# A gather ring of eight blocks whose slots also hold the relation one-hots

## The reference

```python
x = x + _L0_gnn_ref(_layernorm(x), relvectors, w_ih, w_hh, b_ih, b_hh, src, dst, edge_type_16)
x = x + _L0_ffn_ref(_layernorm(x)[None], ...)[0]
x = x + _L1_gnn_ref(_layernorm(x), W, b, edge_index)
x = x + _L1_ffn_ref(_layernorm(x)[None], ...)[0]
```

## Time and profile before

| what | us |
|---|---|
| median of three runs | 3529.81 |
| the profiled execution's own time | 3538.93 |
| its span, first to last instruction | 3537.4 |
| setup, to the first gather | 143.0 |
| layer 0, first to last gather | 143.0 to 1587.5 |
| layer 1, first to last gather | 1691.1 to 2716.2 |
| from the last gather to the end | 821 |

### The profile page before, as it was taken

How to read it: one execution, slowest core, us unless ns; L and a number is a source line. 1 busy time by engine, 2 the same in 40 slices (tenths; PEclk the granted TensorE clock), 3 DMA queues, 4 the chain that set the end, 5 groups by cost and what they waited for, 6 DMA issues and landing times. The chain is left out here.

```text
span 3537.4 us, 56704 instructions
## 1 busy us (share of the span) xinstructions
PE 2454.6 (69%) x14176; PEld 1894.3 (54%) x14177; DVE 1507.1 (43%) x3886; ACT 767.8 (22%) x1370; POOL 1839.2 (52%) x2044
## 2 busy tenths in 40 slices
PE   1288888888877666546577766654444799999991
PEld 1265555555555453324355544333222699999991
DVE  5544444444453342313466454442311544555545
ACT  1222222222222111002111100000000345444450
POOL 0243334444555566770777777777775344444440
PEclk7578788788777776557677776666555899999996
DMA  5321122122222223330433333333332222211116
GB/s 136 97 62 50 52 59 71 58 69 70 82 76 79 82 83 95 102 101 9 116 109 109 102 113 107 107 107 101 110 104 83 80 66 67 67 58 62 54 44 227
DMA packets 157788, 302.92 MB, mean 86 GB/s; under 512 B 47333, under 2 KB 91784, under 8 KB 157720
## 3 DMA queue, kind: packets, MB, share of 16 engines
q0 software_dynamic: 85984, 234.74, 22.9%
q1 hardware_dynamic: 40876, 36.11, 3.4%
q10 hardware_dynamic: 30860, 31.40, 2.7%
HBM read 261.73 MB, written 40.39 MB: 85 GB/s over the span
## 5 line engine op out<-in xcount | busy, mean ns | idle before, releaser
L733 POOL DMA_INDIRECT rows<-table,srcT x1568 | 1536.5, 980 | 942.8 <-issue 465.7
L793 PE MATMUL bank<-rows,onehot 128*128 x3904 | 794.2, 349 | 673.7 <-POOLq L726 553.7
L793 PEld LDWEIGHTS bank<-rows,onehot 128*128 x3904 | 417.8, 113 | 908.6 <-issue 780.2
L759 DVE SCALAR_TENSOR_TENSOR onehot<-iota_row,tbase,dstT 128x512 f16 x488 | 367.2, 754 | 639.5 <-PE bank L793 225.9
L1733 PE MATMUL bank<-xe_high,W_high 128*128 128x256 f32 x864 | 252.7, 292 | 30.2 <-DVE xe_low L1811 30.0
L1783 ACT ACTIVATE hid<-bank,b 128x256 f32<-128x256 f32 x432 | 181.8, 472 | 346.6 <-PE bank L1735 346.4
L1734 PE MATMUL bank<-xe_low,W_high 128*128 128x256 f32 x864 | 250.7, 290 | 0.0
L1735 PE MATMUL bank<-xe_high,W_low 128*128 128x256 f32 x864 | 250.3, 290 | 0.0
L1819 DVE TENSOR_TENSOR hid_low<-hid,hid_high 128x512 fp32r<-128x512 f32 x216 | 149.7, 693 | 235.9 <-ACT hid_high L1787 235.9
L1733 PE MATMUL bank<-W_high,hid_high 128*128 128x256 f32 x864 | 248.3, 287 | 0.0
L1735 PE MATMUL bank<-W_high,hid_low 128*128 128x256 f32 x864 | 243.8, 282 | 0.0
(11 more groups left out here) (340 smaller groups left out, 3744.1 us busy)
## 6 DMA issues: line engine op xcount, KB each, us to landing
rows<-table,srcT POOLq DMA_INDIRECT x1568, 2.8
W<-in_L_ffn_W_dram SPq DMA_DIRECT2D x14, 1024.0 KB, 7.4
y<-results ACTq DMA_DIRECT2D x12, 1024.0 KB, 10.0
x_res<-in_x_dram SPq DMA_DIRECT2D x1, 6144.0 KB, 44.1
table<-part ACTq DMA_DIRECT2D x12, 512.0 KB, 3.2
normal<-xn ACTq DMA_DIRECT2D x12, 512.0 KB, 3.4
out_dram<-x_res SPq DMA_DIRECT2D x12, 512.0 KB
table<-part SPq DMA_DIRECT2D x6, 512.0 KB, 2.9
```

What stands on the lines that cost most here:

```text
L733: nc.gpsimd.indirect_dma_start(out=rows[:, k % (M * U), :], out_offset=None, in_=q.table, in_offset=bass.IndirectOffsetOnAxis(srcT[:, k:k ...
L759: last = nc.vector.scalar_tensor_tensor(onehot[:, ds(slot, U), :], iota_row[:, :].unsqueeze(1).to_broadcast([P, U, P]), base, dstT[:, ds(k ...
L793: last = nc.tensor.matmul(sums, hot, ring_rows[:, ds(row0 + (s * PARTS + part_) * D, D)], start=False, stop=False, skip_group_check=True)
```

## The change

1. **The ring of gathered rows holds eight blocks** in both layers: `M` goes from 4 to 8. The number of landing semaphores stays 4 (`LANDED`). `PASS`, the length of the table of frees, is rounded up to 208 from 200.
2. **A slot of layer 0 is wider.** Each chunk's place is 512 elements of rows plus two fields of 16: `PITCH` = 544. The gather writes the first 512. DVE writes the type one-hots into the first field, right behind the low half, or, where the window's first block is one that the window before it has filled already, into the second field, which nobody reads. The tile `typehot` is gone; `typeT` is fp16 in place of fp32; the source tile `ctT` moves into `work`.
3. **PE does two products a chunk in layer 0**, of 256 and of 272 columns. The second adds the low half to the sums and the types to the counts. L796 is gone.

```diff
-M = 4
+M = 8
 MH = 8
+LANDED = 4
-PASS = BLOCKS + M
+PASS = -(-(BLOCKS + M) // M) * M
+ROW = PARTS * D
+PITCH = ROW + 2 * RELS
...
-        typeT = sb("typeT", [P, KCOLS], F32, graph)
+        typeT = sb("typeT", [P, KCOLS], F16, graph)
...
-            return (sb(f"rows{n}", [P, M * U, PARTS * D], F16, where),
+            return (sb(f"rows{n}", [P, M * U, (PITCH, ROW)[n]], F16, where),
...
-        typehot = sb("typehot", [P, MH * U, RELS], F16, layer0)
...
-                self.landed = [sem(f"{name}_rows_landed{m}") for m in range(M)]
+                self.pitch = PITCH if with_types else ROW
+                self.landed = [sem(f"{name}_rows_landed{m}") for m in range(LANDED)]
...
-                            out=rows[:, k % (M * U), :], out_offset=None, in_=q.table,
+                            out=rows[:, k % (M * U), 0:ROW], out_offset=None, in_=q.table,
...
+            opening = window_first(dve, t)
+            before = dve.snap(opening + t)
...
+                    first_use = 1 if j0 > 0 or isinstance(t, int) and t == 0 else (j + (MH - 1)) // MH
+                    at = dve.snap(ring(dve, dve.snap(opening + j), M) * (PITCH // RELS) + (PITCH // RELS - 1) - first_use)
+                    at = narrow(at, 0, ((M - 1) * U + 1) * (PITCH // RELS) - 1)
                     last = nc.vector.tensor_tensor(
-                        typehot[:, ds(slot, U), :], iota_row[:, 0:RELS].unsqueeze(1).to_broadcast([P, U, RELS]),
+                        types[:, ds(at, U, PITCH // RELS), :],
+                        iota_row[:, 0:RELS].unsqueeze(1).to_broadcast([P, U, RELS]),
...
-                    for part_ in range(PARTS):
-                        last = nc.tensor.matmul(sums, hot, ring_rows[:, ds(row0 + (s * PARTS + part_) * D, D)],
-                                                start=False, stop=False, skip_group_check=True)
-                    if q.with_types:
-                        last = nc.tensor.matmul(counts, hot, types[:, ds(type0 + s * RELS, RELS)],
+                    for at, cols in ((0, D), (D, width)):
+                        last = nc.tensor.matmul(acc[:, 0:cols], hot, ring_rows[:, ds(row0 + (s * q.pitch + at), cols)],
                                                 start=False, stop=False, skip_group_check=True)
...
-        ctT = sb("ctT", [RELS, W], F32, layer0)
+        ctT = work[0:RELS, 0, :]
```

More of the change, by code:

```diff
@@ L66, in program @@
 def program(nc, a, out):
-    assert NT == GROUPS * GW + 1 and EP * EJ * P >= NE and BLOCKS % M == 0 and PASS % M == 0
+    assert NT == GROUPS * GW + 1 and EP * EJ * P >= NE and BLOCKS % LANDED == 0 and M == MH and PASS % M == 0
     def narrow(value, low, high):
@@ L724, in ready @@
                 def ready(i, blocks):
-                    pool.wait_ge(q.landed[i % M], p * (BLOCKS // M * 16 * U) + (i // M + 1) * (16 * U))
+                    pool.wait_ge(q.landed[i % LANDED],
+                                 p * (BLOCKS // LANDED * 16 * U) + (i // LANDED + 1) * (16 * U))
                     pool.sem_inc(q.rows_ready, blocks)
@@ L733, in pool_chunks @@
                         nc.gpsimd.indirect_dma_start(
-                            out=rows[:, k % (M * U), :], out_offset=None, in_=q.table,
-                            in_offset=bass.IndirectOffsetOnAxis(srcT[:, k:k + 1], axis=0)).then_inc(q.landed[i % M], 16)
+                            out=rows[:, k % (M * U), 0:ROW], out_offset=None, in_=q.table,
+                            in_offset=bass.IndirectOffsetOnAxis(srcT[:, k:k + 1], axis=0)).then_inc(q.landed[i % LANDED], 16)
                     if i > 0:
@@ L749, in dve_onehots_of @@
         def dve_onehots_of(dve, q, t, j0, j1):
-            before = dve.snap(window_first(dve, t) + t)
+            opening = window_first(dve, t)
+            before = dve.snap(opening + t)
             first = dve.value_load(windows[0:1, ds(t + 2 * NT, 1)], min_val=0, max_val=PASS)
             base = tbase[:, ds(t, 1)]
+            if q.with_types:
+                types = rows[:, :, :].rearrange("p s (c r) -> p (s c) r", r=RELS)
             def block_onehots(j):
@@ L775, in pe_window @@
             blocks = pe.value_load(windows[0:1, ds(t + NT, 1)], min_val=1, max_val=PASS + 1)
-            ring_rows, hots, types = (ring_[:, :, :].rearrange("p s d -> p (s d)") for ring_ in (rows, onehot, typehot))
-            sums, counts = acc[:, 0:D], acc[:, D:D + RELS]
+            ring_rows, hots = (ring_[:, :, :].rearrange("p s d -> p (s d)") for ring_ in (rows, onehot))
             width = D + RELS if q.with_types else D
@@ L784, in pe_window @@
                 slot, hot_slot = ring(pe, m, M), ring(pe, n, MH)
-                row0 = narrow(pe.snap(slot * (PARTS * D)), 0, (M - 1) * U * PARTS * D)
+                row0 = narrow(pe.snap(slot * q.pitch), 0, (M - 1) * U * q.pitch)
                 hot0 = narrow(pe.snap(hot_slot * P), 0, (MH - 1) * U * P)
-                type0 = narrow(pe.snap(hot_slot * RELS), 0, (MH - 1) * U * RELS) if q.with_types else None
                 pe.wait_ge(q.hot, n + 1)
@@ L791, in pe_window @@
                     hot = hots[:, ds(hot0 + s * P, P)]
-                    for part_ in range(PARTS):
-                        last = nc.tensor.matmul(sums, hot, ring_rows[:, ds(row0 + (s * PARTS + part_) * D, D)],
-                                                start=False, stop=False, skip_group_check=True)
-                    if q.with_types:
-                        last = nc.tensor.matmul(counts, hot, types[:, ds(type0 + s * RELS, RELS)],
+                    for at, cols in ((0, D), (D, width)):
+                        last = nc.tensor.matmul(acc[:, 0:cols], hot, ring_rows[:, ds(row0 + (s * q.pitch + at), cols)],
                                                 start=False, stop=False, skip_group_check=True)
                 last.then_inc(q.used, 1)
-            nc.tensor.matmul(sums[:, 0:RELS], zlhs, zrhs[:, 0:RELS], start=False, stop=True,
+            nc.tensor.matmul(acc[:, 0:RELS], zlhs, zrhs[:, 0:RELS], start=False, stop=True,
                              skip_group_check=True).then_inc(q.done, 1)
```

## The result

The change takes 3493.73 us at the median of four runs (3490.52 to 3499.09), against 3528.96 (3520.11 to 3531.26) before: a ratio of 0.990, 95% interval 0.9886 to 0.9913. That is 35 us faster. The forecast was 3408, that is 122 us less, with a range of 3368 to 3452. The sign came true; the size did not, and the measured time lies outside the range.

The account below looks back on a forecast made before the run. The bound was taken to change with place: PE and DVE in layer 0 up to 1033.4 us, POOL after and in layer 1. Terms 96 + 13 + 0 + 13 = 122 us off 3529.81 gave 3408 us, range 3368 to 3452.

Parts of the forecast that it names:

- ring of eight, layer 0: Layer 0: eight slots gain 96 us from 1033.4 us on and 13 us in the windows just before.
- ring of eight, layer 1: Layer 1: POOL's 20.6 us of waits for PE nearly vanish, a gain of 13 us.
- The ring gives 96 behind 1033.4: Layer 0 from 1033.4 us on: 20 us from four blocks issued earlier, 76 from POOL's waits for PE.
- If POOL never stops again: Condition for the 96 us in layer 0 from 1033.4 us on: POOL gathers without stopping for PE.
- Two products: 0: Layer 0: 0.56 us saved a block where PE's sequencer sets the pace, but no net gain in the sum.
- all of it lies under POOL: Layer 0 from 1033.4 us on: PE's saving from two products is hidden because POOL sets the pace.
- Two more sequencer instructions, 0.12 us each: 1.17 us a use: DVE's one-hot loop in layer 0: two added steps bring the period from 0.93 to 1.17 us a use.
- the sum of 0: Layer 0 up to 936 us: PE's shorter windows and DVE's longer steps cancel; bounds -35 to +25 us.
- rival 2: DVE becomes layer 0's bound at 1.4 us a use or more: +25 to 936, 96 shrinks by 20; 3453 us, chance 0.14.
- Layer 1, the types' width, `ctT`, the pitch: Layer 1 gains 13 us; fp16 types, `ctT` in `work` and the wider row spacing each under 1 us either way.
- rival 4: Gathers get longer beside DVE's one-hots and ring writes: 150 ns more each gives 3580 us, slower; chance 0.04.
- rivals 1: Layer 0: DVE's two steps hide behind its engine, so shorter products come through: -35 more, 3373 us; chance 0.13.

Follow-up runs that it names:

- ring_alone: The kernel before with only the ring of eight blocks and the room made for it (fp16 types, `ctT` in `work`): 3431.28 us, ratio 0.9718.
- products_ring: The kernel before with the ring of eight and PE's two products; DVE still writes types to `typehot`, relation types not counted: 3404.48 us, ratio 0.9646.
- shift_92: The change with 92 semaphore increments ahead of DVE's loops, putting its loop of 349 instructions into three pieces: 3455.46 us, ratio 0.9791.
- types_slot_shift_100: The change with types written at the one-hots' own slot in the unread field (shorter steps, types not counted), plus 100 semaphore increments: 3424.23 us, ratio 0.9691.
- steps_alone: Kernel before with ring, two products and the change's long place computation, types into an unread tile, loop in three pieces: 4177.19, 4170.06, 4179.09 us on slower chips.
- pad_forty: The change with 40 semaphore increments put before DVE's loops of layer 0: 3495.28 us, ratio 0.9908.

## Why the forecast was wrong

| term | forecast | measured | by |
|---|---|---|---|
| ring of eight, layer 0 | 96 + 13 | 101 | window times, *ring_alone* |
| ring of eight, layer 1 | 13 | 15 | gathers' first to last start, *ring_alone* |
| both, by the medians | 122 | 98 | *ring_alone* |
| two products for three | 0 | 27 | *products_ring* to *ring_alone* |
| DVE's register steps (and writes) | 0 | -51 | *shift_92* to *products_ring* |
| instruction fetch at the turn | not seen | -38 | change to *shift_92* |

A plus is a gain. The last four rows sum to 35 before rounding (98 + 27 - 51 - 38). The profiled spans of before and *ring_alone* differ by 115, the medians by 98; the profiled executions lie 10 us above and 7 below their medians, which is why the first rows sum to more.

- **"The ring gives 96 behind 1033.4": right in mechanism, too large by a fifth.** "If POOL never stops again" was the condition, and it did stop for 32.4 us. What was lost there came back in part ahead of it: 26 instead of 13.
- **"Two products: 0" failed.** The step was right up to window 37, which opens only 1 us sooner than with the ring alone. It failed in "all of it lies under POOL". At the windows of 5 to 7 blocks behind it, shorter blocks paid: window 45 opens 19.5 us sooner than with the ring alone, the gathers' waits for PE from window 37 on fall from 32.4 to 17.4 us, and the last gather comes 13 sooner. I had called that stretch POOL's as a whole, while its first part was still PE's in turns.
- **"Two more sequencer instructions, 0.12 us each: 1.17 us a use" failed, and with it the sum of 0.** I counted instructions and gave each the mean of the loop. But what stands there now holds a remainder, products and a division, and its two long steps last 0.22 and 0.24 us. The period is 1.39, the end of the range, where rival 2 has DVE as the bound. That rival's price, 25 us to 936 and 20 behind, made 45; measured are 51 with the writes and the increments, of which 31 are shown to be the steps' (*shift_92* to *types_slot_shift_100*).
- **The code's place was missing altogether.** I said of the steps only what they take, never that they lengthen a loop of 337 instructions that ran close to what DVE keeps. The page before had the line to ask about, the 53 packets of q14; nothing in it tells, though, how near the edge the loop was.
- **Layer 1, the types' width, `ctT`, the pitch: right.** Gathers kept their 981 ns, so rival 4 did not happen, and the two-sided access that it feared cost nothing that can be seen here.
- **Rival 2's mechanism was the right one to fear**, with 3453 as its time and a chance of 0.14. With it and the fetch, 3453 + 38 is 3491. That this comes within 3 us is luck in part, as the ring's and the products' errors cancel.

The Trainium skill (TensorE: Matmul & The Clock Gate, Back-to-back issue gap) gave the 976 products an estimated 20 us. The trace's rows were read as speaking against it, and the chip gave 27 by the medians and 17 by the spans. That the size is near doesn't show that mechanism: in the four-block window above it is the sequencer's pace that got shorter, and nearly all of the gain came behind window 37.

Two slips of arithmetic, on which nothing hangs: the chances of the forecast and of rivals 1 and 2, all of them faster, sum to 0.92 and not 0.94, and the range ends at 3452 where rival 2 has 3453.

Left open: how the 20 us that remain of the 51 divide between writes into the ring, the last 0.08 us a use and the increments themselves, since *steps_alone* can't tell.

## What to carry to other kernels

Before a register expression goes into a loop that an engine's own sequencer paces, look up how long its kind lasts in the trace (here 0.04 to 0.14 us for most, 0.22 to 0.24 for one that holds several operations), not how many instructions it is. A change that adds code to a long loop also moves and lengthens that loop: compare the packets of the instruction queue and the gap behind the loop's branch before and after, and try a shift by a few dozen empty instructions before blaming the change. Take a change of several parts apart on the chip: here one part alone gave 98 us, and the whole 35.

## What the runs showed of the hardware that I had not expected

- DVE fetches part of its loop of 337 to 361 instructions anew at each turn, or not, by where the loop lies. The stop is 2.8 to 4.2 us a turn, five packets of 8192 bytes each time. All ten traces from the jobs with 3530 us before, and the kernel before shifted, agree with three pieces of 128 for layer 0. For layer 1's loop of 312 only that a shift of 40 brings the stop is shown: the count of places that fits layer 0 would give it a stop in the change, where there is none, and none in *pad_forty*, where there is one.
- A wait of 3 us of PE can cost up to twice its length when products of 512 columns in fp32 follow: the granted clock is 0.50 for the next 5 to 8 us (0.85 in place of 0.47 us a pair). Where the clock fell in the stopped kernel alone, the window behind came 4.2 to 5.3 us later, elsewhere 3.4 and less, for stops 2.5 to 3.1 us longer.
- The same program can take 18% longer in another job on another chip (4163 against 3530 us), with register steps of about 0.7 us on the sequencers of PE and DVE, and a change that is worth 2 to 3% on one can be worth nothing there.
